# Two more chunks turned by TensorE in a shared bank, a shorter warm-up and a last chunk in pieces, in a feed-forward, attention, feed-forward kernel

## The reference

```
x = x + 0.5 * ffn(layernorm(x))
x = x + attention(layernorm(x))
x = x + 0.5 * ffn(layernorm(x))
```

## Time and profile before

| | us |
|---|---|
| median of 3 runs (lowest, highest) | 170.85 (170.81, 171.0) |
| the profiled execution's own time | 170.79 |
| its span | 169.0 |
| TensorE busy | 160.3 |
| VectorE busy | 136.8 |
| ScalarE busy | 124.3 |
| GpSimd busy | 83.5 |

### The profile page before, as it was taken

The page is one execution under the profiler, slowest core; times in us unless marked ns, Lnnn a source line. Parts: engine busy times, 40 slices in busy tenths (PEclk is TensorE's granted clock), DMA queues, the critical chain, the costliest instruction groups (busy, mean ns, idle before and its releaser), DMA issues.

```text
span 169.0 us, 3429 instructions
## 1 busy us (share of the span) xinstructions
PE 160.3 (95%) x1052; PEld 141.7 (84%) x1052; DVE 136.8 (81%) x442; ACT 124.3 (74%) x249; POOL 83.5 (49%) x101
## 2 busy tenths in 40 slices
PE   6997999999999999899999998899999999999993
PEld 6975898989798999577988786788997899899893
DVE  1799988899899948989999999999997679943121
ACT  3299958987968497699959768989898575756320
POOL 5345527319814898948972880882760039100000
PEclk9999999999999999999999999999999999999999
DMA  4990417066430144421331161423236616036403
GB/s 107 321 285 7 127 64 186 22 198 160 170 81 4 64 141 169 132 59 50 138 98 30 64 190 67 113 71 105 87 126 206 189 45 186 2 123 192 124 21 103
DMA packets 31409, 19.55 MB, mean 116 GB/s; under 512 B 2608, under 2 KB 28448, under 8 KB 31392
## 3 DMA queue, kind: packets, MB, share of 16 engines
q1 hardware_dynamic: 31104, 19.34, 38.4%
q10 hardware_dynamic: 288, 0.00, 0.1%
HBM read 11.94 MB, written 7.40 MB: 114 GB/s over the span
## 4 chain that ended last, share of the span: by engine, by line
PE 75%; DVE 8%; ACT 7%; issue 5%; DMA 2%; POOL 1%; DVEq 0%; ACTq 0%; POOLq 0%
PE quad L804 33%; PE quad L788 9%; PE quad L789 8%; PE quad L790 8%; PE quad L821 3%; PE quad L823 3%; PE quad L822 3%; PE ps_t L858 3%; ACT xn L480 3%; PE ps_g L839 2%; DMA scale<-in_rows_dram 2%; ACT gl L520 2%; PE ps_g L804 1%; DVE ex L706 1%; PE ps_r L828 1%
## 5 line engine op out<-in xcount | busy, mean ns | idle before, releaser
L804 PEld LDWEIGHTS quad<-w2e,gl 128*128 128x128 f32 x496 | 60.2, 192 | 3.2 <-ACT gl L520 0.4
L804 PE MATMUL quad<-w2e,gl 128*128 128x128 f32 x496 | 60.8, 275 | 0.0
L520 ACT ACTIVATE gl<-quad,cols 128x512 f32<-128x512 f32 x64 | 42.6, 682 | 16.6 <-PE quad L790 15.5
L411 POOL TENSOR_TENSOR rstd<-veps,mhalf 128x4 f32<-128x4 f32 (+1 forms) x16 | 16.6, 1043 | 29.1 <-DVE veps L132 29.0
L788 PE MATMUL quad<-xh,w1h 128*128 128x512 f32 x64 | 28.5, 445 | 0.4 <-ACT gl L520 0.2
L480 ACT ACTIVATE xn<-X,nmr,rstd 128x128 f32<-128x128 f32 x61 | 25.0, 486 | 3.5 <-DVE nmr L592 3.5
L789 PE MATMUL quad<-xl,w1h 128*128 128x512 f32 x64 | 25.2, 394 | 0.0
L790 PE MATMUL quad<-xh,w1l 128*128 128x512 f32 x64 | 25.2, 393 | 0.0
L432 POOL TENSOR_TENSOR X<-X,b2h 128x512 f32<-128x512 f32 x16 | 20.6, 1305 | 1.1 <-issue 1.1
L690 DVE TENSOR_TENSOR X<-quad,X 128x512 f32<-128x512 f32 (+1 forms) x16 | 10.7, 672 | 11.7 <-PE quad L804 11.7
L788 PEld LDWEIGHTS quad<-xh,w1h 128*128 128x128 f32 x64 | 12.2, 190 | 2.9 <-issue 1.2
(11 more groups left out here) (105 smaller groups left out, 281.6 us busy)
## 6 DMA issues: line engine op xcount, KB each, us to landing
ev<-token_rows SPq DMA_DIRECT2D x7, 512.0 KB, 4.1
folded<-tq SPq DMA_DIRECT2D x12, 256.0 KB, 2.0
land<-folded SPq DMA_DIRECT2D x48, 64.0 KB, 2.2
folded<-atq SPq DMA_DIRECT2D x8, 256.0 KB, 2.0
aland<-folded SPq DMA_DIRECT2D x32, 64.0 KB, 2.1
X<-in_x_dram SPq DMA_DIRECT2D x7, 256.0 KB, 5.5
out_dram<-X SPq DMA_DIRECT2D x7, 256.0 KB, 2.6
w1t<-in_w1t_dram SPq DMA_DIRECT2D x1, 256.0 KB, 3.5
```

What stands on the lines that cost most here:

```text
L411: pool.tensor_tensor(rstd[:, i, own], veps[:, i, own], mhalf[:, own], ALU.pow).then_inc(s_rstd, 1)
L520: act.activation(gl[:, f % 2, j], ps_h[j % 2], ACT.Gelu, bias=cols[:, j:j + 1]).then_inc(s_gelu, 1)
L804: ins = pe.matmul(y[:, n * P:(n + 1) * P], gl[:, f % 2, j, n * P:(n + 1) * P], w2e[:, f // PER_B % 2, j], start=(j == 0), stop=(j == HB - 1))
```

## The change

`PE_TURNS` gets chunks 8 and 9. They are turned in `ps_t`, which attention's outputs use at that time: `turn.8` stands after `o.4` and `turn.9` after `o.6`, each waits until VectorE has read that output, and `o.5` and `o.7` wait in turn until ScalarE and VectorE have read the turned chunk (`s_lo`) and VectorE the odd rows (`s_od`). `blocks`, `put` and `land` of 8 and 9 go. The warm-up becomes one group of 11, inside `lead`. The last chunk is added and stored in three pieces of 2, 1 and 1 tiles; the third tile goes to `ps_g`, the fourth to `ps_r`, and the last store is issued by ScalarE. The orders of all five engines are written anew. At the start VectorE's `rest.0` and `stats.1` now precede `norm.0`, and `stats.2` and `norm.1` precede `odd.0`. `qk.0.0` and `qk.0.1` precede `down.7`.

```diff
-WARM_UP = (11, 4, 4)
+WARM_UP = 11
+LAST = [slice(0, 2), slice(2, 3), slice(3, 4)]
-PE_TURNS = (0, 1, 2, 3)
+PE_TURNS = (0, 1, 2, 3, 8, 9)
+AFTER = {8: 5, 9: 7}
...
 dve order, start
-scale.0 stats.0 moments.0 norm.0 rest.0 stats.1 rest_norm.0 odd.0 moments.1 first_w1.0 first_w1.1 stats.2
+scale.0 stats.0 moments.0 rest.0 stats.1 norm.0 moments.1 rest_norm.0 stats.2 norm.1 odd.0 moments.2 first_w1.0
 act order, start
-norm.0 rest.0 first_w1h.0 first_w1h.1 turn.0 first_w1h.2 first_w1h.3 norm.1 up.0.0 up.0.1 turn.1 norm.2
+norm.0 rest.0 norm.1 turn.0 first_w1h.0 first_w1h.1 first_w1h.2 norm.2 turn.1 up.0.0 first_w1h.3 up.0.1
 act order, from exp.7.1 on
+exp.7.1 norm.9 gram.7 turn.8 qturn.5 norm.10 w1h.4 mix.3.1 qturn.6 norm.11 up.8.0 up.8.1 turn.9 up.8.2
 dve order, from feat.7.1 on
+feat.7.1 moments.10 norm.9 o.4 moments.11 z.6 z_sums.7 norm.10 turn.8 mix.3.0 odd.4 norm.11 w1.4 blocks.10
+o.5 w1l.4 z.7 stats.12 stats.13 o.6 w2.4 turn.9
 pe order, around the end of the first feed-forward
-down.7.0 down.7.1 down.7.2 down.7.3 qk.0.0 qk.0.1 qk.0.2 qk.0.3
+qk.0.0 qk.0.1 down.7.0 down.7.1 down.7.2 down.7.3 qk.0.2 qk.0.3
 pe order, end of attention
-mix.2.0 mix.2.1 gram.6 o.4 qturn.5 gram.7 up.8.0 mix.3.0 o.5 up.8.1 qturn.6 mix.3.1 up.8.2 up.8.3 o.6 qturn.7 up.9.0
+mix.2.0 qk.7.0 qk.7.1 qk.7.2 qk.7.3 qturn.4 mix.2.1 o.4 gram.6 gram.7 turn.8 qturn.5 mix.3.0 o.5 qturn.6
+mix.3.1 up.8.0 o.6 up.8.1 qturn.7 turn.9 up.8.2 up.8.3 up.9.0
...
+        def y_of(f, n):
+            return [ps_y[f % 2], ps_y[f % 2], ps_g, ps_r][n] if f == FC - 1 else ps_y[f % 2]
...
 turn (TensorE)
-                    if i == CHUNKS:
-                        pe.wait_ge(s_x2, CHUNKS - 4)
+                    if i in AFTER:
+                        pe.wait_ge(s_x2, AFTER[i])
...
 o (TensorE)
                     wait(pe, s_x2, i)
+                    for f, n in AFTER.items():
+                        if n == i:
+                            pe.wait_ge(s_lo, f + 1)
+                            pe.wait_ge(s_od, f // PER_B + 1)
...
 down (VectorE)
+                    for tiles in LAST if f == FC - 1 else [slice(0, NT)]:
+                        dve.wait_ge(s_d, NT * f + tiles.stop)
...
+                if stage == "last":
+                    act.wait_ge(s_x3, CHUNKS - 1 + len(LAST))
+                    act.dma_start(chunk_of(out, CHUNKS - 1)[:, LAST[-1]], X[:, CHUNKS - 1, LAST[-1]]).then_inc(s_out, 16)
```

More of the change, by code:

```diff
@@ L375, in _ @@
                     c = i[0] - CHUNKS
-                    parts = 2 if c == CHUNKS - 1 else 1
-                    for h in range(parts):
-                        tiles = slice(NT // parts * h, NT // parts * (h + 1))
+                    for h, tiles in enumerate(LAST[:-1] if c == CHUNKS - 1 else [slice(0, NT)]):
                         sp.wait_ge(s_x3, c + h + 1)
                         sp.dma_start(chunk_of(out, c)[:, tiles], X[:, c, tiles]).then_inc(s_out, 16)
-            sp.wait_ge(s_out, 16 * (CHUNKS + 1))
+            sp.wait_ge(s_out, 16 * (CHUNKS - 1 + len(LAST)))
         @block.gpsimd
@@ L684, in _ @@
                     dve.wait_ge(s_xb, f + 1)
-                    parts = 2 if f == FC - 1 else 1
-                    for h in range(parts):
-                        tiles, part = NT // parts, TOK // parts
-                        dve.wait_ge(s_d, NT * f + tiles * (h + 1))
-                        dve.tensor_tensor(flat(X[:, to, tiles * h:tiles * (h + 1)]),
-                                          (ps_g if h == 1 else ps_y[f % 2])[:, part * h:part * (h + 1)],
-                                          flat(X[:, to, tiles * h:tiles * (h + 1)]), ALU.add).then_inc(
-                            s_x1 if f < CHUNKS else s_x3, 1)
+                    for tiles in LAST if f == FC - 1 else [slice(0, NT)]:
+                        dve.wait_ge(s_d, NT * f + tiles.stop)
+                        dve.tensor_tensor(flat(X[:, to, tiles]), y_of(f, tiles.start)[:, D * tiles.start:D * tiles.stop],
+                                          flat(X[:, to, tiles]), ALU.add).then_inc(s_x1 if f < CHUNKS else s_x3, 1)
                 if stage == "head sums":
@@ L742, in _ @@
                     pe.transpose(ps_g[:, 0:D], wb[:, 2], ident[:]).then_inc(k_wv, 1)
-                if stage == "warm up":
-                    if i[1] == 0:
-                        pe.wait_ge(k_id, 1)
-                    for n in range(WARM_UP[i[1]]):
-                        pe.matmul(ps_h[1][:, 0:P], ident[:], ident[:], start=True, stop=True)
                 if stage == "turn":
@@ L764, in _ @@
                 if stage == "lead":
+                    pe.wait_ge(k_id, 1)
+                    for n in range(WARM_UP):
+                        pe.matmul(ps_h[1][:, 0:P], ident[:], ident[:], start=True, stop=True)
                     pe.wait_ge(s_xn, 1)
@@ L800, in _ @@
                         wait(pe, s_x3, f - 1 - CHUNKS)
-                    y = ps_g if f == FC - 1 and n >= NT // 2 else ps_y[f % 2]
+                    if f == FC - 1 and n == 2:
+                        pe.wait_ge(s_x2, CHUNKS)
+                        pe.wait_ge(m_gs, NB)
+                    y = y_of(f, n)
                     for j in range(HB):
```

## The result

The changed kernel takes 172.75 us (172.16 to 173.41, 4 runs) where the kernel before took 170.83 beside it (170.25 to 171.0, 4 runs): ratio 1.0123, 95% interval 1.0089 to 1.0157. It is slower, as forecast (171.5), by 1.9 us and not by 0.65. Its four runs fell at 172.2 and 173.4 us, two each, and the profiled one took 173.34; its span is 171.3, 2.3 more than that of before.

A forecast was written before the change was run, and what follows sets the result against it. Bounds: latency at the start, TensorE's work in both feed-forwards, full VectorE in attention. +0.2 - 0.4 + 1.5 - 0.45 - 0.2 = +0.65 on 170.79 gave 171.45, median 171.5 us; own range 170.7 to 172.3, 8 in 10 169.6 to 173.0.

The forecast's parts named there:

- the rival in which the clock falls: TensorE's clock at 1.2 GHz for the first blocks after the shorter warm-up: +1 to +2 us, 173.0; chance 0.13.
- Start, +0.2: Start of the kernel: shorter warm-up saves nothing, VectorE's new order delays the first blocks; +0.2 us, bounds -0.3 and +1.0.
- First feed-forward, -0.4: First feed-forward: same work, but paired up blocks make the needed gelu older; -0.4 us, bounds -0.8 and 0.
- the waits near 40 us: First feed-forward: three small TensorE waits that sum, with the slower starts after them, to about 0.8 us.
- Attention, +1.5: Attention through up.9.3: VectorE's queue sets up.8.0; +1.2 us from the queue count plus 0.3 for VectorE meeting GpSimd.
- the port: Attention: VectorE operations slowed beside GpSimd ones at moments.9 and moments.11; +0.3 us, bounds 0 and 0.9.
- the waiting term, 3.1: Attention: waiting in VectorE's new queue before w1l.4, 3.1 us (bounds 2.1 and 3.9), against 2.1 in the old.
- Second feed-forward, -0.45: Second feed-forward: VectorE and ScalarE stay ahead, so the stall before 130.56 and small ones go; -0.45 us, bounds -0.6 and 0.
- End, -0.2: End: last addition falls from 0.42 to about 0.26 us, last store halves; -0.2 us, bounds -0.4 and +0.2.
- relief: Rival: VectorE's removed work reaches TensorE, attention costs less than +0.5 us; total 170.2 or 169.6; chance 0.28.

The follow-up runs named there:

- the tail alone: Kernel before with only the last chunk in pieces of 2, 1 and 1 tiles, last store issued by ScalarE: 170.09 us, ratio 0.9989.
- the old order until attention: Changed kernel with the old order of all engines up to the end of down.7.3, then the new one: 173.28 us, ratio 1.0175.
- by DRAM: Changed kernel with its order, but chunks 8 and 9 turned by block transposes and DRAM again: 175.26 us, ratio 1.0284.
- the halves: Two changed-kernel variants: old order until attention, then new (173.28 us); new order until 71 us, then old, chunks 8 and 9 through DRAM (172.59 us).
- the control: The changed kernel once more, unaltered, timed beside the kernel before: 172.54 us, ratio 1.0131.
- the old start: Changed kernel with the old order of all engines up to about 24 us, then the new one, short warm-up kept: 172.5 us, ratio 1.0102.
- the late turns: Kernel before with the last chunk in three pieces and chunks 8 and 9 turned by TensorE after o.4 and o.6: 177.9 us, ratio 1.0408.

## Why the prediction was right, and what was mis-sized

The direction and the mechanism were right: in attention the removed VectorE work does not reach TensorE, since `turn.8`, `odd.4`, `w1.4` and `w1l.4` now stand in a row before `up.8.0`. The size was not. The forecast's own range was 170.7 to 172.3, and 172.75 lies above it. The wide range reached 173.0 only for the rival in which the clock falls, which the profiled execution does not show, so that it held is in part luck. The prediction also called itself wrong if the first stretch came out over 1 us off; with the first feed-forward in it, it did (+1.05 against -0.2). By its steps:

- **Start, +0.2.** The order's part is right as far as it can be told. `norm.0` ran at 6.89 (forecast 6.9), `up.0.0` at 12.44 (12.6), `up.1.0` at 16.27 (16.5), and taking the start back changed nothing. The eight multiplications removed were put at nothing because they stood in pauses. Removed alone they cost 1.4 us, none of it at the start. No run gives the new order its old warm-up back, so how much of the 1.9 us is theirs is not shown. The places where that run lost time, `land.8` and the second feed-forward, are not places where the changed kernel lost any: it has no `land.8` and gained behind `up.9.3`.
- **First feed-forward, -0.4.** This step failed, sign included: with the start at +0.2 it measured +0.85. Part of the gain was not there to be had: the waits near 40 us, taken at 0.8, are 0.60 in the trace that the forecast was read from and 0.15 in that of the tail alone. And the forecast looked at TensorE's own pieces and did not follow VectorE and GpSimd there:

```profile
43.11 1.73 DVE L630 TENSOR_TENSOR xl<-land,xh 128x512 fp32r<-128x512 f32 x1
44.76 1.25 DVE L650 TENSOR_TENSOR od<-land,scl 128x8 f32<-128x8 f32 x1
...
49.07 1.14 DVE L657 SCALAR_TENSOR_TENSOR w1r<-ev,od,w1t 128x128 f32<-128x128 f32 x4
...
51.02 1.05 DVE L673 TENSOR_TENSOR w1l<-w1r,w1h 128x512 fp32r<-128x512 f32 x1 [0.19 <-ACT w1h L512]
...
43.01 2.97 POOL L439 TENSOR_TENSOR X<-X,b2h 128x512 f32<-128x512 f32 x2
...
50.26 2.96 POOL L439 TENSOR_TENSOR X<-X,b2h 128x512 f32<-128x512 f32 x2
```

w1l.3 ends at 52.07, and `up.6.0` starts at 52.18. Five items stand between `odd.3` and `w1.3` where the old order had one. In six executions with this order `up.6.0` starts 0.1 us after w1l.3 ends (51.0 to 53.1), and from the start of `odd.3` to the end of w1l.3 7.3 to 7.5 us pass; in the kernel before it is 4.6. That time is the order's and not the 1.25 us of `odd.3` above: it is the same in the three of the six where `odd.3` takes 0.16. The new order's rate is also read from more than one trace: less the 1.40, `down.7.3` starts at 65.6 to 66.8 in five executions that have it, mean 66.35, and at 65.2 to 66.1 in seven with the old, mean 65.45.
- **Attention, +1.5.** Measured +2.36. From the end of `down.7.3`'s slot (69.1) to `up.8.0` it took 45.7 us, where 44.4 had been forecast before the port's 0.3. The rest, `up.8.0` to the end of `up.9.3`, took 8.7 (forecast 9.0, of which the items by their own slots sum to 8.3 and not to 8.6). The mis-sized term is the port, taken at 0.3 with a bound of 0.9. The same 128x4 operation that takes 0.17 without a neighbour:

```profile
71.40 0.63 DVE L137 TENSOR_SCALAR aveps<-amv 128x4 f32<-128x4 f32 x1
...
89.36 0.32 DVE L137 TENSOR_SCALAR veps<-mv 128x4 f32<-128x4 f32 x1
...
96.18 0.77 DVE L137 TENSOR_SCALAR veps<-mv 128x4 f32<-128x4 f32 x1
...
95.64 1.28 POOL L444 TENSOR_TENSOR X<-X,rows 128x512 f32<-128x512 f32 x1
```

Three times VectorE ends within 0.03 us of its neighbour on GpSimd (the last at 96.95 beside 96.92), which costs 0.46 + 0.15 + 0.60 = 1.2 us of its queue; the forecast had named `moments.9` (the last) rightly, `moments.11` wrongly (0.17), and not the first two. In the old order all five such rows between `down.7.3` and `up.8.0` take 0.17, and the stretched veps row comes after it. The Trainium skill (SBUF — State Buffer, section Who interferes with whom) calls this an exclusive lock; by that rule, blocking to the neighbour's end, the addition was 0.9, and the trace agrees with it rather than with the 0.3. It is read from the ends of the rows; no run moved GpSimd alone. How much of the 1.2 reaches TensorE is not shown either: with the old order until attention the first of the three rows takes 0.17, and `up.8.0` comes only 0.3 earlier. If all of it does, the waiting term, 3.1, holds within 0.2; VectorE's idle time between `down.7.3` and `up.8.0` is 1.98 us (1.63 before), so the waiting hardly grew.
- **Second feed-forward, -0.45.** Measured -0.71, and no stall stands after 125 us, as forecast. From `up.9.3` to `down.15.3` five further executions with the new order there take the same 45.0, the one by DRAM 47.6; with the old order it is 45.5 to 45.7, and 46.3 and 46.5 in the two that have the short warm-up.
- **End, -0.2.** Measured -0.4 in the trace; 0.2 in the times of the tail alone. The last addition, on 128 columns:

```profile
168.10 0.29 DVE L698 TENSOR_TENSOR X<-ps_g,X 128x128 f32<-128x128 f32 x1 [0.40 <-PE ps_g L809]
169.00 0.29 DVE L698 TENSOR_TENSOR X<-ps_r,X 128x128 f32<-128x128 f32 x1 [0.60 <-PE ps_r L809]
```

The rivals: relief did not come, attention cost 2.4 us and not under 0.5. The clock did not fall in the profiled execution, so it is not the cause of its loss; it did fall in others, below.

What stays open: why the shorter warm-up alone costs 1.4 us against the kernel before without any mark at the start, how much of the changed kernel's loss is its, how the halves' 2.3 and 3.0 us become 2 together, and why the turns as placed cost 7.6 us in the old order when the changed kernel, which has them in the same place, loses 1.9 in all.

## What to carry to other kernels

When work is moved into a slot where the data it starts from is there anyway, count the whole chain that hangs on it down to its last consumer: here 5.1 to 5.6 us from the turn to `up.8.0`, which cost nothing that the times tell with the turn 13 us ahead, and 3.7 us by `up.8.0` at the place chosen, in the old order. A region whose work doesn't change still needs its queues followed when their order does, on every engine; the stall will be where one engine's late item is another's operand. And one stall mended in a full hand-written order came out at a later item in both runs that tried it: an edit of the order is priced by its time, not by the stall that it removes.

## What the hardware showed unexpectedly

The granted clock of TensorE dropped to its lower level (1.2 GHz) for 3.4 us in four of the twelve profiles of experiments, at places that differ. Windows of the control, of the old start and of the run by DRAM; that of the late turns (0.52) is shown above:

```profile
8.60:10.70 2.10, 2.10 (x11) 2.10 (x12) 1.79 (x13) 2.10 (x6) 1.25 (x2) 0.50 1.12 319
```

```profile
52.80:56.00 3.20, 2.90 (x8) 2.35 (x9) 3.17 (x10) 1.30 (x4) 2.85 (x4) 0.56 0.60 184
```

```profile
13.00:16.00 3.00, 3.00 (x9) 2.17 (x7) 2.32 (x14) 2.10 (x5) 1.06 (x2) 0.53 0.07 21
```

All four followed a stop of TensorE: in the control 2.68 us before 8.47, with the old start 2.04 before 53.10 (the records there stand 0.43 us apart), by DRAM 1.81 before `turn.1` at 12.03, with the late turns 1.17 and 1.62 in turn. The changed kernel's profile has stops of 1.80 (before the same `turn.1`), 1.49 and 1.39 and no such drop, so the length of the stop alone does not decide it. In the control the drop cost nothing by `down.7.3`; `select` and the turn ran at half the rate beside ScalarE and VectorE that were behind as well.

The stretched VectorE rows are more regular than the clock. In the 14 traces 99 operations on 128x4 or 128x8 elements start while GpSimd has at least 0.25 us left of an operation on 128x512. Of these 94 end 0.02 to 0.03 us after it, the longest after 1.25 us in place of 0.16. The other five take their 0.16: they are `odd.4` in runs that turn chunk 8 late, which reads the chunk from the PSUM bank `ps_t` and not from `land`. Rows beside GpSimd's `stats` (the power, 128x4) are not stretched.
